# Second layer of an attention and Mamba block: dt goes through DRAM to the decay instead of through TensorE

## The chip, the core and the metric
The kernel runs on one core of one Trainium2 chip. The metric is the device time of one execution in microseconds. The core has five engines with instruction streams of their own: TensorE (PE, matmuls; its weight loads are listed as PEld), VectorE (DVE), ScalarE (ACT), GpSimd (POOL), and SyncE (SP), which here only issues DMA transfers. They are ordered among each other by semaphores. PSUM is the memory that TensorE writes, in 8 banks of 128 partitions x 512 float32; SBUF is the large on-chip memory.

## The reference
Input x is (4, 128, 64, 64) float32. Layer 0 is attention over the 4096 pixels with 4 heads, a residual and a layer norm; its result is z. Layer 1 adds a 3x3 convolution, a spectral convolution (FFT, 1x1, inverse FFT) and a Mamba block over the pixels as a sequence. The change touches the Mamba block:

```
xi, z = split(in_proj_w @ u);  xs = silu(conv1d(xi))          # 256 channels
dt = softplus(dt_proj_w @ x_dbl[:8] + dt_proj_b)              # 256 channels
A = -exp(A_log)                                               # 256 x 16 states
h = exp(dt * A) * h + dt * B * xs                             # for each channel and state, over 4096 positions
y = sum over states of h * C, + xs * D;  out = out_proj_w @ (y * silu(z))
```

## The kernel before
Layer 0 fills the first part of the time, layer 1 the rest; they don't overlap. Layer 1 (the function `layer1`) cuts each of the 4 images into 8 chunks of 512 positions, so it has NIT = 32 steps. In a step the recurrence is worked off in G = 32 groups. A group holds 8 channels x 16 states on the 128 partitions: partition p has channel p // 16 and state p % 16.

For each group g of step `it`:

- TensorE repeats each channel's u = dt * xs on its 16 partitions with a selection matrix, into one of NU = 3 PSUM banks (`repeat_u`, L995), and dt likewise into the single bank DT_BANK (`repeat_dt`, L988), LEAD = 4 groups ahead. Both read a split form: `s_dt` and `s_u` hold a high part and the rest, one on each half of the partitions, in a rounded float32 format, so that one pass of each suffices.
- ScalarE makes the decay `d_a` = exp(a_neg * dt) from DT_BANK into a ring of NDA = 8 tiles (`decay`, L1103). It also copies the last state of group g - 6 into `carry` (L1094), which waits for that group's scan.
- VectorE multiplies u by B in PSUM (`times_b`, L1175), one group ahead of the scan, and then scans (L1189): hh = d_a * hh + that product, along the 512 positions.
- GpSimd multiplies hh by C (L1218), and TensorE sums the states of 4 groups at a time (`sum_states`, L972).

Between the groups of step `it`, the functions `prepare(it + 1, ...)` of each engine work out the inputs of the next step, each piece at a fixed group number written out by hand. For dt on ScalarE: relu and abs in groups 19 and 20, Exp in 21, Ln in 22. On VectorE: dt = relu + ln in group 20 (semaphore `dt_sum`), ux = dt * xs in group 21. The split is made by `high` on ScalarE (L1045) and `low` on VectorE (L1140), in groups 25 and 26 for dt, 27 and 28 for u. In group 10 ScalarE makes two silus between two loads of its function table (L1039, L1040), having waited until VectorE has added the last half of the step before (`y_added`, VectorE's group 5). The convolutions and the output projection are further matmuls on TensorE in the gaps (`fill`, `fill_g`, `out_proj`).

The order on each engine is the order of the code. On TensorE a group is: repeat_u(g), prepare, sums and fills, repeat_dt(g + 4). repeat_dt waits until the decay of the group before has read DT_BANK (`da_ready`), repeat_u until the scan three groups back has freed its bank (`scanned`). The first two steps are written out, the other 30 run in a hardware loop of two steps. SP loads the chunk z of step it + 2 once TensorE has finished with the buffer (`z_used`, group 28 of step it), and stores each finished output; it too has a loop.

Of the kernel before, what the change touches and what calls it, by code (L numbers as in the profile page):

```python
# [673 lines left out]
ST = 16  # L674
GC = 128 // ST
INNER = 2 * C
# [8 lines left out]
def layer1(nc, z_ext, w, out, nb=B):  # L685
# [13 lines left out]

    NIT = nb * STEPS  # L700
    with ExitStack() as ctx:
        def sb(name, shape, dt=F32):
# [9 lines left out]
        ps = ctx.enter_context(nc.psum_tensor("ps1", [128, 8, CH], F32))  # L712
        DT_BANK, U_BANK, Y_BANK, O_BANK, ITEM_BANK = 0, 1, 4, 5, 6
        NU = 3
        win = sb("win", [C, 2 * INNER])
# [23 lines left out]
        gz = sb("gz", [128, 2, 2, LC])  # L739
        s_dt = sb("s_dt", [128, 2, 4, LC], F32R)  # L740
        s_u = sb("s_u", [128, 2, 4, LC], F32R)
# [10 lines left out]
        yt = sb("yt", [128, 2, LC])  # L752
        NDA, NHH, NHC = 8, 8, 8
        d_a = sb("d_a", [128, NDA, LC])
# [7 lines left out]
        with nc.Block() as block:  # L762
# [27 lines left out]
            def _(dve):  # L790
# [23 lines left out]
        (z_in, flipped, item, item_read, sp_log, dt_sum, u_prod, hi_ready, lo_ready,  # L814
         dt_rep, u_rep, da_ready, bu_ready, scanned, kept, hc_ready, y_done, y_added, gated, z_used, o_ready, o_copied,
         o_full, o_even, o_odd) = [sem(x) for x in (
             "z_in", "flipped", "item", "item_read", "sp_log", "dt_sum", "u_prod",
             "hi_ready", "lo_ready", "dt_rep", "u_rep", "da_ready", "bu_ready", "scanned", "kept", "hc_ready", "y_done",
             "y_added", "gated", "z_used", "o_ready", "o_copied", "o_full", "o_even", "o_odd")]


        XS, XD, DT, BI, CI, GATE, GI, NITEM = 0, 2, 3, 5, 6, 7, 9, 10
        G = GROUPS
        LEAD = 4

# [10 lines left out]

        def u_bank_free(it, g):

            before = g - NU if g >= NU else max(k for k in range(G) if k % NU == g % NU) - G
            return it * G + before + 1  # L840

# [11 lines left out]
        with nc.Block() as block:  # L853
            @block.sync
            def _(sp):
                def load(j, p):

                    jw = j if isinstance(j, int) else j % NIT
                    b, lc = jw // STEPS, jw % STEPS

                    ge(sp, z_used, j - 1)
                    ge(sp, flipped, 2 * j)
                    sp.dma_start(za[:, p, :], z_ext[b, :, bass.ds(lc * LC, HALO)]).then_inc(z_in, 16)
                    sp.dma_start(zp[:, p, :, 1:W + 1], z_ext[b, :, bass.ds(lc * LC, HALO)].rearrange("c (h w) -> c h w", w=W)).then_inc(z_in, 16)

                    last = (STEPS - 1 - lc) * LC + W
                    sp.dma_start(stage_j[:, 0:ROWS - 1, :], z_ext[b, :, bass.ds(last + W, LC - W)].rearrange("c (h w) -> c h w", w=W)).then_inc(z_in, 16)
                    sp.dma_start(stage_j[:, ROWS - 1, :], z_ext[b, :, bass.ds((STEPS - lc) % STEPS * LC + W, W)]).then_inc(z_in, 16)

                def store(j, p):  # L870
                    b, lc = j // STEPS, j % STEPS
                    sp.wait_ge(o_full, j + 1)
                    sp.dma_start(out[b, :, bass.ds(lc * LC, LC)], o_sb[:, p, :]).then_inc((o_even, o_odd)[p], 16)

                load(0, 0)
                load(1, 1)
                load(2, 0)
                with sp.Fori(1, NIT // 2) as k:
                    store(k * 2 - 2, 0)
                    load(k * 2 + 1, 1)  # L880
                    store(k * 2 - 1, 1)
                    load(k * 2 + 2, 0)
                store(NIT - 2, 0)
                store(NIT - 1, 1)

                sp.wait_ge(o_even, 16 * (NIT // 2))
                sp.wait_ge(o_odd, 16 * (NIT // 2))
                sp.wait_ge(z_in, 64 * (NIT + 1))

            @block.tensor  # L890
            def _(pe):
# [90 lines left out]

                def repeat_dt(it, p, g):
                    s, j = column(g)
                    if g == 0:
                        pe.wait_ge(lo_ready, it * 4 + 2)
                    ge(pe, da_ready, it * G + g)
                    nc.tensor.matmul(ps[:, DT_BANK, :], sel_g[:, j, :], s_dt[:, p, s, :], start=True, stop=True).then_inc(dt_rep, 1)  # L988

                def repeat_u(it, p, g):  # L990
                    s, j = column(g)
                    if g == 0:
                        pe.wait_ge(lo_ready, it * 4 + 4)
                    ge(pe, scanned, u_bank_free(it, g))
                    nc.tensor.matmul(ps[:, U_BANK + g % NU, :], sel_g[:, j, :], s_u[:, p, s, :], start=True, stop=True).then_inc(u_rep, 1)  # L995
# [3 lines left out]
                def emit(it, p):  # L999
                    for g in range(G):  # L1000
                        if isinstance(it, int) and it == g == 0:
                            for d in range(LEAD):
                                repeat_dt(it, p, d)
                        repeat_u(it, p, g)
# [10 lines left out]
                        if g >= 8 and g % 4 == 0:  # L1015
                            sum_states(it, g // 4 - 2)
                        if g + LEAD < G:
                            repeat_dt(it, p, g + LEAD)
                        else:
                            repeat_dt(it + 1, 1 - p, g + LEAD - G)  # L1020

# [8 lines left out]
            def _(act):  # L1030
# [16 lines left out]
                def prepare(j, p, g):  # L1047
# [12 lines left out]
                    elif g in (19, 20):  # L1060

                        h = g - 19
                        if h == 0:

                            ge(act, lo_ready, j * 4)
                        nc.scalar.activation(dt[:, h, :], take(j, DT + h), ACT.Relu, bias=cols[:, 2 + h:3 + h])
# [9 lines left out]
                    elif g in (25, 26):  # L1076
                        act.wait_ge(dt_sum, j + 1)
                        high(j, p, s_dt, dt, g - 25)
                    elif g in (27, 28):
                        act.wait_ge(u_prod, j + 1)  # L1080
                        high(j, p, s_u, ux, g - 27)
                    elif g == 29:
# [41 lines left out]
                def tail():  # L1124

                    for g in range(LEAD - 1):
                        decay(NIT, g)
                    for g in range(G - KEEP, G):
# [6 lines left out]
            def _(dve):  # L1135
                def low(j, p, stack, src, part, n):

                    a, b = slice(64 * part, 64 * part + 64), slice(64 - 64 * part, 128 - 64 * part)
                    dve.wait_ge(hi_ready, j * 4 + 2 * n + part + 1)
                    nc.vector.tensor_tensor(stack[b, p, part::2, :], src[a, :, :], stack[a, p, part::2, :].bitcast(F32), ALU.subtract  # L1140
                                            ).then_inc(lo_ready, 1)

                def prepare(j, p, g):
# [161 lines left out]
```

## Time and profile before

| | us |
|---|---|
| median of 3 runs | 6361.38 (6359.47 to 6361.48) |
| profiled execution | 6361.27 |
| its span, first to last instruction | 6359.3 |
| mean granted TensorE clock | 0.955 of 2.4 GHz |
| TensorE busy in the span | 5868.1 (92%) |
| VectorE busy | 5011.0 (79%) |
| GpSimd busy | 4188.6 (66%) |
| ScalarE busy | 3777.6 (59%) |

The profile is one execution recorded by the hardware. An engine's busy time is the sum of its instructions without overlap; the difference to the span is idle time. For each idle stretch the profile names what ended it, inferred from the semaphores. Shares over the whole span mix the two layers, so the numbers that matter here are those of the second layer alone, which a window in time gives.

### The profile page before, as it was taken

Reading aid. Unit: us, or ns where it says so; the run is one execution under the profiler, and the core shown is the slowest. Engines: PE = TensorE matmul, PEld = TensorE weight load, DVE = VectorE, ACT = ScalarE, POOL = GpSimd, SP = SyncE. Lnnn points to the kernel's source line nnn. Section 1 sums busy time; section 2 is a strip of 40 time slices with the busy share of each in tenths; the row PEclk is TensorE's granted clock in tenths of the full one; section 3 lists DMA queues with packets and bytes.
Section 4 is the critical chain, followed back from the end, with each engine's and each line's share of the span. In section 5 each row is a group of like instructions: output and inputs, shape, how many; then the busy total and the mean of one; then the engine's idle time right before and its main releaser. Section 6 shows DMA issues by size and latency. Waiting matters only on the chain. (4 is left out here: it accounts for less than half of the span.)

```text
span 6359.3 us, 93797 instructions
## 1 busy us (share of the span) xinstructions
PE 5868.1 (92%) x28212; PEld 2757.3 (43%) x28212; DVE 5011.0 (79%) x7254; ACT 3777.6 (59%) x7359; POOL 4188.6 (66%) x3147
## 2 busy tenths in 40 slices
PE   7999999999999999999999997888888888888887
PEld 3444444444444444444444442333333333333333
DVE  7777777777777777777777773798999998899988
ACT  3666566656666666666666665655556655556655
POOL 2677766776666776666677764566666666666666
PEclk9999999999999999999999998898989998889988
DMA  4011011011011011011000001000000000000000
GB/s 128 22 38 41 26 32 41 25 41 42 26 32 36 29 42 39 27 32 31 14 21 22 9 17 41 15 22 16 15 15 17 15 21 15 15 15 17 15 21 11
DMA packets 143428, 175.15 MB, mean 28 GB/s; under 512 B 64832, under 2 KB 88256, under 8 KB 141504
## 3 DMA queue, kind: packets, MB, share of 16 engines
q1 hardware_dynamic: 142944, 169.73, 9.4%
q8 instruction: 178, 2.92, 0.2%
q14 instruction: 306, 2.51, 0.1%
HBM read 109.11 MB, written 58.98 MB: 26 GB/s over the span
## 5 line engine op out<-in xcount | busy, mean ns | idle before, releaser
L560 POOL TENSOR_TENSOR sums<-exps 128x512 f32<-128x512 f32 x2048 | 2620.2, 1302 | 1309.9 <-ACT exps L493 1305.2
L569 DVE TENSOR_REDUCE mpart<-ps 128x1 f32<-128x512 f32 x4096 | 2539.8, 682 | 820.7 <-PE ps L369 820.7
L493 ACT ACTIVATE exps<-ps 128x512 f32<-128x512 f32 x4096 | 2127.8, 602 | 1404.5 <-PE ps L376 1404.1
L1218 POOL TENSOR_TENSOR hc<-hh,c_rep 128x512 f32<-128x512 f32 x1024 | 1490.0, 1458 | 825.8 <-DVE hh L1189 824.9
L369 PE MATMUL ps<-k_st,q_ring 96*128 96x512 f32 x4096 | 1753.7, 429 | 19.0 <-DMA k_st<-qk_split 9.4
L376 PE MATMUL ps<-q_ring,k_st 98*128 98x512 f32 x4096 | 1621.0, 397 | 4.0 <-ACT exps L493 3.6
L1189 DVE TENSOR_TENSOR_SCAN hh<-d_a,carry,ps 128x512 f32<-128x512 f32 x1024 | 1297.6, 1270 | 2.1
L369 PEld LDWEIGHTS ps<-k_st,q_ring 96*128 96x128 f32 x4096 | 774.7, 189 | 1065.6 <-DVE mpart L569 529.4
L1103 ACT ACTIVATE d_a<-ps,a_neg 128x512 f32<-128x512 f32 x1027 | 706.6, 688 | 726.3 <-PE ps L988 688.3
L387 PE MATMUL ps<-exps,v_ring 128*32 128x512 f32 x8192 | 1090.8, 605 | 0.0
L988 PE MATMUL ps<-s_dt,sel_g 128*128 128x512 f32 x1028 | 638.6, 621 | 324.0 <-ACT d_a L1103 319.7
L1175 DVE TENSOR_TENSOR ps<-ps,b_rep 128x512 f32<-128x512 f32 x1024 | 698.1, 682 | 216.7 <-PE ps L995 201.2
L376 PEld LDWEIGHTS ps<-q_ring,k_st 98*128 98x128 f32 x4096 | 778.0, 190 | 148.3 <-ACT exps L493 17.3
L988 PEld LDWEIGHTS ps<-s_dt,sel_g 128*128 128x128 f32 x1028 | 215.8, 210 | 973.8 <-ACT d_a L1103 747.4
L995 PE MATMUL ps<-s_u,sel_g 128*128 128x512 f32 x1024 | 467.0, 456 | 72.6 <-DVE hh L1189 72.5
L399 PE MATMUL ps<-sums,ones_d 128*32 128x512 f32 x4096 | 533.1, 592 | 0.0
L387 PEld LDWEIGHTS ps<-exps,v_ring 128*32 128x32 f32 x8192 | 161.2, 108 | 416.2 <-ACT exps L493 362.0
L908 PE MATMUL ps<-za,wtap 128*128 128x512 f32 x528 | 285.9, 637 | 28.6 <-DMA stage_j<-z_ext 28.6
L972 PE MATMUL ps<-hc,sel_y 128*32 128x512 f32 x2048 | 299.9, 660 | 4.6 <-POOL hc L1218 4.6
L995 PEld LDWEIGHTS ps<-s_u,sel_g 128*128 128x128 f32 x1024 | 223.1, 218 | 166.1 <-DVE hh L1189 114.2
L954 PE MATMUL ps<-zp,wconv 128*128 128x512 f32 x576 | 278.3, 592 | 0.0
L399 PEld LDWEIGHTS ps<-sums,ones_d 128*32 128x32 f32 x4096 | 133.0, 110 | 306.6 <-issue 296.8
(110 smaller groups left out, 3409.0 us busy)
## 6 DMA issues: line engine op xcount, KB each, us to landing
qk_split<-hilo SPq DMA_DIRECT2D x128, 256.0 KB, 2.3
q_ring<-qk_split SPq DMA_DIRECT2D x384, 64.0 KB, 2.0
k_st<-qk_split SPq DMA_DIRECT2D x45, 512.0 KB, 7.2
za<-z_ext SPq DMA_DIRECT2D x33, 320.0 KB, 3.1
zp<-z_ext SPq DMA_DIRECT2D x33, 320.0 KB, 4.0
xc<-in_x SPq DMA_DIRECT2D x32, 256.0 KB, 3.0
v_dram<-v_stage SPq DMA_DIRECT2D x32, 256.0 KB, 2.3
v_ring<-v_dram SPq DMA_DIRECT2D x16, 512.0 KB, 3.8
```

Source lines behind the costliest of these rows:

```text
L369: nc.tensor.matmul(d_bank(("max", m, t)), q_ring[0:PARTS, m % 4, 128 * i:128 * i + 128], k_st[0:PARTS, g % 2, chunk(kc)], start=True, stop ...
L376: nc.tensor.matmul(a_bank(("exp", n, t)), k_st[0:SHIFT, n // NCH % 2, 128 * t:128 * t + 128], q_ring[0:SHIFT, n % 4, :], start=True, stop= ...
L387: ins = nc.tensor.matmul(ps[D * i:D * i + D, OUT_BANK, :], v_ring[:, n // NCH % 2, 4 * v + i, :], exps[:, (2 * v + i // 2) % 4, CH * (i % ...
L493: nc.scalar.activation(exps[:, u % 4, CH * half:CH * half + CH], a_bank(("exp", n, t)), ACT.Exp, scale=SCALE).then_inc(a_done, 1)
L560: pool.tensor_tensor(sums[:, u % 8, :], exps[:, u % 4, 0:CH], exps[:, u % 4, CH:2 * CH], ALU.add).then_inc(summed, 1)
L569: nc.vector.tensor_reduce(mpart[:, m % 2, t % 4, t // 4:t // 4 + 1], d_bank(("max", m, t)), AX.X, ALU.max).then_inc(d_done, 1)
L988: nc.tensor.matmul(ps[:, DT_BANK, :], sel_g[:, j, :], s_dt[:, p, s, :], start=True, stop=True).then_inc(dt_rep, 1)
L995: nc.tensor.matmul(ps[:, U_BANK + g % NU, :], sel_g[:, j, :], s_u[:, p, s, :], start=True, stop=True).then_inc(u_rep, 1)
L1103: nc.scalar.activation(d_a[:, g % NDA, :], ps[:, DT_BANK, :], ACT.Exp, scale=a_neg[:, s * 8 + j:s * 8 + j + 1]).then_inc(da_ready, 1)
L1175: nc.vector.tensor_tensor(bu, bu, b_rep[:, p, :], ALU.mult).then_inc(bu_ready, 1)
L1189: nc.vector.tensor_tensor_scan(hh[:, g % NHH, :], d_a[:, g % NDA, :], ps[:, U_BANK + g % NU, :], carry[:, it % STEPS, s * 8 + j:s * 8 + j ...
L1218: pool.tensor_tensor(hc[:, g % NHC, :], hh[:, g % NHH, :], c_rep[:, p, :], ALU.mult).then_inc(hc_ready, 1)
```

## The change
dt no longer goes through TensorE. When VectorE has made the dt of a step (all 256 channels x 512 positions), SP stores it to a DRAM tensor `dt_dram` with two halves, one for each parity of the step (`store_dt`). For each group SP then loads the 8 channels of that group back, each channel to 16 neighbouring partitions, straight into the tile of `d_a` that the decay will use (`load_dt`); ScalarE's Exp works in place there. The ring `d_a` grows from 8 to 16 tiles, with one semaphore for each tile. The load for group g + 16 is issued when the scan of group g is done; SP's program is written out in full for this, without a loop, with the z loads at group 26 and the output store at group 18. `repeat_dt`, its PSUM bank, `s_dt` and its `high` and `low` parts go away; u gets a fourth PSUM bank, and its split moves to groups 25 and 26. `repeat_u` then waits for the scan four groups back.

```diff
-        DT_BANK, U_BANK, Y_BANK, O_BANK, ITEM_BANK = 0, 1, 4, 5, 6
-        NU = 3
+        U_BANK, Y_BANK, O_BANK, ITEM_BANK = 0, 4, 5, 6
+        NU = 4
-        NDA, NHH, NHC = 8, 8, 8
+        NDA, NHH, NHC = 16, 8, 8
...
+                def store_dt(j, p):
+                    sp.wait_ge(dt_sum, j + 1)
+                    sp.dma_start(dt_dram[p].rearrange("(h q) l -> q h l", h=2), dt[:, :, :]).then_inc(dt_stored, 16)
+
+                def load_dt(j, p, g):
+                    if g == 0:
+                        sp.wait_ge(dt_stored, j * 16 + 16)
+                    c = channels(g)
+                    sp.dma_start(d_a[:, g % NDA, :], dt_dram[p, c:c + GC, :].rearrange("c (o l) -> c o l", o=1).to_broadcast([GC, ST, LC])
+                                 ).then_inc(dt_in[g % NDA], 16)
+
+                def emit(it, p):
+                    for t in range(G):
+                        if t == G - NDA:
+                            store_dt(it + 1, 1 - p)
+                        sp.wait_ge(scanned, it * G + t + 1)
+                        if t + NDA < G:
+                            load_dt(it, p, t + NDA)
+                        else:
+                            load_dt(it + 1, 1 - p, t + NDA - G)
+                        if t == 18 and it:
+                            store(it - 1, 1 - p)
+                        if t == 26 and it + 2 <= NIT:
+                            load(it + 2, p)
...
-                def repeat_dt(it, p, g):
-                    s, j = column(g)
-                    if g == 0:
-                        pe.wait_ge(lo_ready, it * 4 + 2)
-                    ge(pe, da_ready, it * G + g)
-                    nc.tensor.matmul(ps[:, DT_BANK, :], sel_g[:, j, :], s_dt[:, p, s, :], start=True, stop=True).then_inc(dt_rep, 1)
...
-                    ge(pe, scanned, u_bank_free(it, g))
+                    ge(pe, scanned, it * G + g - NU + 1)
...
-                            ge(act, lo_ready, j * 4)
+                            ge(act, u_prod, j)
+                            ge(act, dt_stored, j * 16)
...
-                        act.wait_ge(dt_sum, j + 1)
-                        high(j, p, s_dt, dt, g - 25)
-                    elif g in (27, 28):
                         act.wait_ge(u_prod, j + 1)
-                        high(j, p, s_u, ux, g - 27)
+                        high(j, p, s_u, ux, g - 25)
...
-                    act.wait_ge(dt_rep, it * G + g + 1)
-                    ge(act, scanned, it * G + g - NDA + 1)
-                    nc.scalar.activation(d_a[:, g % NDA, :], ps[:, DT_BANK, :], ACT.Exp,
+                    act.wait_ge(dt_in[g % NDA], it * (16 * G // NDA) + 16 * (g // NDA) + 16)
+                    nc.scalar.activation(d_a[:, g % NDA, :], d_a[:, g % NDA, :], ACT.Exp,
...
-                        low(j, p, s_dt, dt, g - 25, 0)
-                    elif g in (27, 28):
-                        low(j, p, s_u, ux, g - 27, 1)
+                        low(j, p, s_u, ux, g - 25)
```

## Rows read from the trace of the kernel before

**Rows 1.** The page: the span in 40 slices, VectorE busy and the granted TensorE clock.
```profile
DVE  7777777777777777777777773798999998899988
...
PEclk9999999999999999999999998898989998889988
```
**Rows 2.** Timeline of VectorE (start us, us, engine, line): first and last scan.
```profile
4013.75 1.27 DVE L1189 TENSOR_TENSOR_SCAN hh<-d_a,carry,ps 128x512 f32<-128x512 f32 x1
...
6342.87 2.44 DVE L1189 TENSOR_TENSOR_SCAN hh<-d_a,carry,ps 128x512 f32<-128x512 f32 x2
```
**Rows 3.** Window 4100 to 6200 us: busy (count) of PE, PEld, DVE, ACT, POOL, clock, DMA share, GB/s.
```profile
4100.00:6200.00 2100.00, 1743.10 (x5973) 793.08 (x5971) 1904.23 (x2098) 1243.85 (x2556) 1405.06 (x976) 0.90 0.06 17
```
**Rows 4.** Instruction groups, 4100 to 6200 us: busy us, mean ns, idle before and releaser.
```profile
L1218 POOL TENSOR_TENSOR hc<-hh,c_rep 128x512 f32<-128x512 f32 x919 | 1338.8, 1460 | 693.8 <-DVE hh L1189 692.9 <-PE ps L972 0.9
L1189 DVE TENSOR_TENSOR_SCAN hh<-d_a,carry,ps 128x512 f32<-128x512 f32 x920 | 1165.9, 1270 | 1.9
L1103 ACT ACTIVATE d_a<-ps,a_neg 128x512 f32<-128x512 f32 x919 | 632.3, 688 | 656.0 <-PE ps L988 618.2 <-DVE hh L1189 32.8 <-issue 2.8
...
L988 PE MATMUL ps<-s_dt,sel_g 128*128 128x512 f32 x919 | 572.6, 623 | 292.3 <-ACT d_a L1103 288.3
...
L1140 DVE TENSOR_TENSOR s_dt<-dt,s_dt 64x1024 fp32r<-64x1024 f32 x58 | 70.7, 1220 | 1.8
```
**Rows 5.** Waits, 4100 to 6200 us: us in total, times, longest.
```profile
ACT d_a L1103 <- PE ps L988: 618.2, 630, 4.4
...
DVE ps L1175 <- PE ps L995: 175.9, 142, 2.4
```
**Rows 6.** Timeline of VectorE: scans around an s_dt subtraction, and without one.
```profile
5014.81 1.28 DVE L1189 TENSOR_TENSOR_SCAN hh<-d_a,carry,ps 128x512 f32<-128x512 f32 x1
...
5017.98 1.27 DVE L1189 TENSOR_TENSOR_SCAN hh<-d_a,carry,ps 128x512 f32<-128x512 f32 x1
...
5035.81 1.27 DVE L1189 TENSOR_TENSOR_SCAN hh<-d_a,carry,ps 128x512 f32<-128x512 f32 x1
...
5037.59 1.27 DVE L1189 TENSOR_TENSOR_SCAN hh<-d_a,carry,ps 128x512 f32<-128x512 f32 x1
```
**Rows 7.** Timeline of ScalarE, TensorE, VectorE about group 10; idle time before in brackets.
```profile
5044.90 1.28 ACT L1039 ACT_TABLE_LOAD   x1 [1.54 <-DVE yt L1160]
...
5048.78 0.69 ACT L1103 ACTIVATE d_a<-ps,a_neg 128x512 f32<-128x512 f32 x1
...
5049.52 0.50 PE L988 MATMUL ps<-s_dt,sel_g 128*128 128x512 f32 x1 [3.40 <-ACT d_a L1103]
...
5050.29 0.70 DVE L1175 TENSOR_TENSOR ps<-ps,b_rep 128x512 f32<-128x512 f32 x1 [1.93 <-PE ps L995]
```
**Rows 8.** Timeline of the second layer's start: the dt sum and the first decay.
```profile
3995.37 1.23 DVE L1146 TENSOR_TENSOR dt<-dt,edt 128x1024 f32<-128x1024 f32 x1 [25.57 <-ACT edt L1073]
...
4006.93 0.69 ACT L1103 ACTIVATE d_a<-ps,a_neg 128x512 f32<-128x512 f32 x1
```
**Rows 9.** DMA: a 256 KB load; windows over reads, narrow loads, a store, z loads.
```profile
xc<-in_x SPq DMA_DIRECT2D x32, 256.0 KB, 3.0
...
178.70:184.50 5.80, 5.80 (x37) 2.75 (x37) 4.18 (x9) 3.52 (x8) 4.89 (x4) 1.00 0.27 81
...
329.00:336.00 7.00, 7.00 (x41) 3.39 (x41) 5.76 (x12) 4.46 (x9) 4.96 (x4) 1.00 1.04 223
...
5068.60:5071.60 3.00, 2.98 (x11) 1.21 (x12) 3.00 (x4) 3.00 (x7) 2.32 (x2) 1.00 0.23 87
5091.30:5097.00 5.70, 4.43 (x37) 3.62 (x30) 5.57 (x7) 2.02 (x5) 3.90 (x3) 1.00 0.64 161
```
**Rows 10.** Windows of 2.4 us: the clock (third column from the end) low, and back.
```profile
5101.60:5104.00 2.40, 2.32 (x9) 0.49 (x9) 1.78 (x3) 0.00 (x0) 2.30 (x2) 0.50 0.00 0
...
5108.80:5111.20 2.40, 2.40 (x9) 1.24 (x7) 2.40 (x3) 1.25 (x3) 1.28 (x2) 1.00 0.01 3
```

More of the change, by code:

```diff
@@ L700, in layer1 @@
     NIT = nb * STEPS
+    dt_dram = nc.dram_tensor("dt_dram", [2, INNER, LC], F32, kind="Internal").ap()
     with ExitStack() as ctx:
@@ L739, in layer1 @@
         gz = sb("gz", [128, 2, 2, LC])
-        s_dt = sb("s_dt", [128, 2, 4, LC], F32R)
         s_u = sb("s_u", [128, 2, 4, LC], F32R)
@@ L814, in layer1 @@
         (z_in, flipped, item, item_read, sp_log, dt_sum, u_prod, hi_ready, lo_ready,
-         dt_rep, u_rep, da_ready, bu_ready, scanned, kept, hc_ready, y_done, y_added, gated, z_used, o_ready, o_copied,
-         o_full, o_even, o_odd) = [sem(x) for x in (
+         u_rep, da_ready, bu_ready, scanned, kept, hc_ready, y_done, y_added, gated, z_used, o_ready, o_copied,
+         o_full, o_even, o_odd, dt_stored) = [sem(x) for x in (
              "z_in", "flipped", "item", "item_read", "sp_log", "dt_sum", "u_prod",
-             "hi_ready", "lo_ready", "dt_rep", "u_rep", "da_ready", "bu_ready", "scanned", "kept", "hc_ready", "y_done",
-             "y_added", "gated", "z_used", "o_ready", "o_copied", "o_full", "o_even", "o_odd")]
+             "hi_ready", "lo_ready", "u_rep", "da_ready", "bu_ready", "scanned", "kept", "hc_ready", "y_done",
+             "y_added", "gated", "z_used", "o_ready", "o_copied", "o_full", "o_even", "o_odd", "dt_stored")]
+        dt_in = [sem(f"dt_in{i}") for i in range(NDA)]
         XS, XD, DT, BI, CI, GATE, GI, NITEM = 0, 2, 3, 5, 6, 7, 9, 10
         G = GROUPS
-        LEAD = 4
         def ge(e, s, value):
@@ L835, in column, with channels @@
             return 2 * half + i // 2, jj + 4 * (i % 2)
-        def u_bank_free(it, g):
-            before = g - NU if g >= NU else max(k for k in range(G) if k % NU == g % NU) - G
-            return it * G + before + 1
+        def channels(g):
+            half, jj, i = g // 16, g // 4 % 4, g % 4
+            return 128 * half + 32 * i + GC * jj
         def steps(e, prepare, emit, tail):
@@ L856, in load @@
                 def load(j, p):
-                    jw = j if isinstance(j, int) else j % NIT
+                    jw = j % NIT
                     b, lc = jw // STEPS, jw % STEPS
@@ L873, in store @@
                     sp.dma_start(out[b, :, bass.ds(lc * LC, LC)], o_sb[:, p, :]).then_inc((o_even, o_odd)[p], 16)
+                def store_dt(j, p):
[20 more added lines that the diff above has]
+                            load(it + 2, p)
                 load(0, 0)
                 load(1, 1)
[L877 to L883, printed above, removed]
+                store_dt(0, 0)
+                for g in range(NDA):
+                    load_dt(0, 0, g)
+                for it in range(NIT):
+                    emit(it, it % 2)
                 store(NIT - 1, 1)
@@ L887, in _ @@
                 sp.wait_ge(o_odd, 16 * (NIT // 2))
+                for i in range(NDA):
+                    sp.wait_ge(dt_in[i], 16 * (NIT * G // NDA + 1))
                 sp.wait_ge(z_in, 64 * (NIT + 1))
@@ L992, in repeat_u @@
                     if g == 0:
-                        pe.wait_ge(lo_ready, it * 4 + 4)
-                    ge(pe, scanned, u_bank_free(it, g))
+                        pe.wait_ge(lo_ready, it * 2 + 2)
+                    ge(pe, scanned, it * G + g - NU + 1)
                     nc.tensor.matmul(ps[:, U_BANK + g % NU, :], sel_g[:, j, :], s_u[:, p, s, :], start=True, stop=True).then_inc(u_rep, 1)
@@ L1000, in emit @@
                     for g in range(G):
-                        if isinstance(it, int) and it == g == 0:
-                            for d in range(LEAD):
-                                repeat_dt(it, p, d)
                         repeat_u(it, p, g)
@@ L1016, in emit @@
                             sum_states(it, g // 4 - 2)
[L1017 to L1020, printed above, removed]
                 def tail():
@@ L1124, in tail @@
                 def tail():
-                    for g in range(LEAD - 1):
-                        decay(NIT, g)
                     for g in range(G - KEEP, G):
@@ L1135, in _, with low @@
             def _(dve):
-                def low(j, p, stack, src, part, n):
+                def low(j, p, stack, src, part):
                     a, b = slice(64 * part, 64 * part + 64), slice(64 - 64 * part, 128 - 64 * part)
-                    dve.wait_ge(hi_ready, j * 4 + 2 * n + part + 1)
+                    dve.wait_ge(hi_ready, j * 2 + part + 1)
                     nc.vector.tensor_tensor(stack[b, p, part::2, :], src[a, :, :], stack[a, p, part::2, :].bitcast(F32), ALU.subtract
```

## The prediction

> **What bounds the kernel now.** The change touches only the second layer, so I first looked in the page's forty slices for where that layer lies: from the 26th slice on, where VectorE (DVE) is at 8 to 9 tenths and the granted clock of TensorE at 8 to 9 tenths [rows 1]. The first scan starts at 4013.75 us and the last ends at 6342.87 + 2.44 = 6345.31 us [rows 2]. That is 2331.6 us for 32 steps of 32 groups, 72.86 us a step. Then one window over the steady part, 4100 to 6200 us, which is 2100 / 72.86 = 28.82 steps: DVE is busy for 1904 of 2100 us, TensorE 1743, ScalarE 1244, GpSimd 1405, the DMA engines 6% [rows 3]. Per step that is DVE 66.1 us and 6.8 us idle. So DVE is nearly the bound, but not quite, and the list of waits tells what the rest is: DVE's multiplication by B waits 175.9 us for TensorE's repeat of u, 6.1 us a step, and this is nearly all of its idle time. In the same list ScalarE's decay waits 618 us for TensorE's repeat of dt [rows 5].
>
> The timeline shows how the two hang together. TensorE issues in order: repeat of u for group g, other work, repeat of dt for group g+4. That dt repeat may only start when the decay of g+3 has read the one dt bank. ScalarE makes two table loads and two silus in group 10, so the decay of group 11 comes late, at 5048.78 us. TensorE has stood idle for 3.40 us when its dt repeat starts at 5049.52; the u repeat queued behind it is later still, and DVE's product starts at 5050.29 after 1.93 us of idleness [rows 7]. The decays themselves are far ahead of the scan: no scan waits for one (1.9 us of idle time before 920 scans [rows 4]). DVE waits for u only because u stands in the queue behind dt.
>
> **What the change removes.** (1) On TensorE 32 dt repeats a step of 0.623 us, 19.9 us a step [rows 4]. TensorE isn't the bound, so this counts for nothing by itself; what counts is that the coupling is gone. A u repeat then waits only for the scan four groups back (a fourth bank; three before), while DVE needs it when the scan two groups back ends. That is a margin of two groups, 2 x 1.77 us, against in-line work of mostly 0.9 to 2 us a group.
> (2) On DVE the two subtractions into s_dt. From scan start to scan start takes 5037.59 - 5035.81 = 1.78 us without an extra operation and 5017.98 - 5014.81 = 3.17 us with one s_dt subtraction [rows 6]. So each costs 1.40 us on the path, a little more than its 1.22 us [rows 4], and the two 2.8 us a step. DVE's work a step becomes 66.1 - 2.8 = 63.3 us. This is the floor.
> (3) On ScalarE two casts a step and one of the two waits of each decay. ScalarE is busy 1244 / 28.82 = 43.2 us a step [rows 3]; worth nothing on the path. The Exp reads SBUF in place of PSUM. Bounds for one: 0 and 0.69 us as now [rows 4]; I take it as unchanged, and even +0.1 us on each would leave ScalarE at 46 us.
>
> **What it adds.** (4) On the SP queue 32 loads of 256 KB a step, one store of 512 KB, and a wait for the scan before each load. The load of group g+16 starts when scan g is done; ScalarE can't run more than six groups ahead of the scan (its copies of the last state are in the same stream), so a load has ten groups, some 20 us, to land. A load of 256 KB lands in 3.0 us now [rows 9]. The awkward place is t = 16: the store of the next step's dt stands first there and waits for the dt sum, which DVE makes after scan 20. Queued behind it on SP are the loads of groups 0 to 4 of the next step, and then the wait for the store. They go out in a burst at about scan 21 or 22 and are wanted from scan 31 on; with 3 us for the store, 3 us for the first load and under 2 us for each further one, nothing is late. The z loads now stand at t = 26 behind that scan, where they waited for TensorE's fill of group 28 before. They land 6 us later, when TensorE may stand for some 2 us at group 1 of the next step, inside the margin of (1).
> (5) The DMA engines' throughput is the real unknown, since no row of before has this form: eight rows of 2 KB in DRAM, each written to 16 partitions. Per packet of 2 KB the store of 256 KB took 0.23 x 3.0 us x 16 engines = 11.0 engine-us for 128 packets, 86 ns; the reads from 178.7 us took 0.27 x 5.8 x 16 = 25.1 engine-us for 0.47 MB, 53 us per MB, so 14 engine-us for 256 KB [rows 9]. Spread over 16 engines a load takes 0.69 to 0.88 us, over 8 engines 1.38 to 1.75 us. The low end is 0.69. For the high end I take the loads of 329 to 336 us, whose destinations are 32 partitions only: all engines busy, but 223 GB/s in all, 13.9 GB/s an engine [rows 9]. If only 8 engines work, at this rate, 32.8 KB each take 2.35 us. Beside them the step has the z loads (0.64 x 5.7 = 3.65 us of all engines [rows 9]), the output (0.69) and the dt store (twice that, 1.38): 5.7 us. So the DMA needs 28 to 34 us a step on 16 engines, 50 to 62 on 8, and 81 on 8 that get in each other's way; DVE needs 63.3. I take 50 to 62, under DVE's floor, nearest to the plain reads and stores.
>
> The Trainium skill, page "DMA: Bandwidth & Descriptors", section "Why a DMA increments its semaphore by 16 and not by 1", says that a copy is spread over the largest number up to 16 that divides the slowest dimension of both sides; here these are 8 and 128, so 8 engines. No row here shows such a copy; by that rule 1.38 us and up holds, not 0.69. The page "SBUF — State Buffer", section "Door 1: The DMA port swizzle", says that partitions reach the 16 DMA ports in a pattern, so that a narrow range has only some of them; the trace agrees for the 32-partition loads (223 GB/s). Together they would make the last rival below.
>
> (6) Start: dt is summed at 3995.37 + 1.23 = 3996.60 us and the first decay ran at 4006.93 [rows 8]. Store and first load need about 6 us, so dt is there by about 4003, before ScalarE comes to it. The first scan then no longer waits for five dt repeats and decays in turn; it can start near 4006.9, 7 us earlier than at 4013.75.
>
> **The sum.** The profiled execution took 6361.27 us, its span 6359.3; the median of the runs is 6361.38, the same within 0.1 us. Of the 6.8 us idle a step I leave 0.7: TensorE still falls to 1.2 GHz after idle stretches (0.50 at 5101.6 us [rows 10]) and is then slow for some 7 us, which eats most of the margin of two groups once or twice a step. Step = 63.3 + 0.7 = 64.0 us, saving 8.86 x 32 = 283.5 us, and 7 us at the start: 6361.3 - 290.5 = 6071 us. By itself this case lies between 6045 (no stall left) and 6130 (2.5 us left).
>
> **Rivals.**
> A. The DMA is the bound but still quicker than now: 1.8 to 2.1 us a load, for instance 1.95: 32 x 1.95 + 5.7 = 68.1 us a step, 6361.3 - 7 - 32 x 4.76 = 6202 us. For it: the high end of the plain reads, 1.75 us on 8 engines, is only just below the 1.79 us from which DMA exceeds DVE. Against: the stores at 86 ns.
> B. The DMA makes the kernel slower: 8 engines, each at the 13.9 GB/s of the narrow loads, 2.35 us a load, 81 us a step, and scans then wait for decays and these for loads: 6361.3 - 7 + 32 x 8.1 = 6614 us. It decides from 2.10 us a load on (32 x 2.10 + 5.7 = 72.9), 125 GB/s. For it: each channel goes to 16 neighbouring partitions, so several engines may write at once where the narrow loads met. Against: in one load all 128 partitions are written.
> C. TensorE keeps stalling DVE, by its clock. Without the dt repeats it is busy 60.5 - 19.9 = 41 us of 64, so it idles more and is granted 1.2 GHz for longer; u would then be late as now. Price: the 6.1 us of waits stay, 69.4 us a step: 6361.3 - 7 - 32 x 3.46 = 6244 us. Against: where TensorE is behind it is busy without a gap, and after such a stretch the clock was back: 0.50 from 5101.6 us, 1.00 from 5108.8 us [rows 10].
> GpSimd is no rival: 1.46 us a group [rows 4] against 1.97.
>
> **How the numbers follow.** Forecast 50%, A 15%, C 8%, B 25%, no change (something not seen gives it all back) 2%. The predicted time is 6071. Under 0.2% (13 us) a measurement of this kernel can't tell from no change. Faster: 50 + 15 + 8 = 73%; same 2%; slower 25%. The range runs from 6040 into case B until a fifth is left out, to 6480; the likeliest case's own range is 6045 to 6130.
>
> **What would show it.** Right: no TensorE group that writes ps from s_dt; DVE above 97% busy in the second layer, with scans 64 us x 32 in sum; no wait of a decay for a DMA apart from the start; DVE's wait for u down from 175.9 us to under 30 in the same stretch; a mean DMA share of 0.43 to 0.53 in the second layer ((32 x 11 to 14 + 16 x 5.7) engine-us of 16 x 64). Wrong: ScalarE's decay waiting for d_a from dt_dram and time from issue to landing growing far above 3 us (A or B; the rate tells which), or DVE still waiting for ps of L995's counterpart with a clock at 0.8 or less (C).

## The result, and the profile after

The changed kernel takes 6183.6 us, the median of 4 runs from 6175.5 to 6202.5; the kernel before took 6360.4 beside it. The ratio is 0.9727, with a 95% interval of 0.9704 to 0.9749. That is 177 us less, where 290 were forecast: the way and the stated range (6040 to 6480) are right, but the time lies outside the likeliest case's own range (6045 to 6130). It lies in the stated range only because that was stretched for rivals A to C, and none of them came about: that part is luck. The profiled execution took 6181.0 us, its span 6179.2.

The page of the changed kernel, its span in 40 slices: VectorE, the granted TensorE clock, the DMA engines.
```profile
DVE  7777777777777777777777777299999999999998
PEclk9999999999999999999999999899899889988998
DMA  4011011111110110110100000244444444444444
```
VectorE now shows 9 tenths nearly throughout the second layer (8 and 9 in [rows 1]), and the DMA engines 4 tenths.

The timeline of the changed kernel's VectorE (start, us, engine, line): first and last scans.
```profile
4006.75 1.27 DVE L1195 TENSOR_TENSOR_SCAN hh<-d_a,carry,ps 128x512 f32<-128x512 f32 x1
...
6162.16 2.44 DVE L1195 TENSOR_TENSOR_SCAN hh<-d_a,carry,ps 128x512 f32<-128x512 f32 x2
```
The first scan is 7.0 us earlier than in [rows 2]. Between the ends lie 6164.60 - 4006.75 = 2157.9 us, 67.43 us a step; before it was 72.86. So 32 x 5.43 + 7.0 = 181 us, which is the whole difference of the two profiled executions (6361.3 - 6181.0 = 180).

The window of the steady part, 4100 to 6000 us (898 scans, so 28.06 steps of 67.7 us), its columns as in [rows 3], and then its costliest groups.
```profile
4100.00:6000.00 1900.00, 1459.61 (x4938) 592.63 (x4940) 1774.28 (x1993) 1165.38 (x2441) 1313.06 (x954) 0.90 0.45 150
```
```profile
L1224 POOL TENSOR_TENSOR hc<-hh,c_rep 128x512 f32<-128x512 f32 x898 | 1246.8, 1392 | 587.3 <-DVE hh L1195 584.9 <-PE ps L999 2.4
L1195 DVE TENSOR_TENSOR_SCAN hh<-d_a,carry,ps 128x512 f32<-128x512 f32 x898 | 1136.6, 1268 | 0.9
L1113 ACT ACTIVATE d_a<-d_a,a_neg 128x512 f32<-128x512 f32 x898 | 642.0, 720 | 76.0 <-issue 74.6
L1181 DVE TENSOR_TENSOR ps<-ps,b_rep 128x512 f32<-128x512 f32 x898 | 605.9, 678 | 123.1 <-issue 64.2 <-PE ps L1016 57.6
```
VectorE is busy 1774.28 / 28.06 = 63.2 us a step; 63.3 was forecast. The idle time is where the forecast fails: 125.7 / 28.06 = 4.5 us a step, not 0.7. The list of waits of the same window (total us, times, longest) divides it, and shows who else waits.
```profile
ACT s_u L1059 <- DVE ux L1157: 154.4, 28, 5.6
PE ps L935 <- DMA stage_j<-z_ext: 146.7, 28, 8.1
ACT zj L1066 <- DMA stage_j<-z_ext: 131.5, 28, 7.5
...
ACT d_a L1113 <- issue: 74.6, 13, 6.2
DVE ps L1181 <- issue: 64.2, 19, 4.9
...
DVE ps L1181 <- PE ps L1016: 57.6, 39, 5.1
```
The decays no longer wait for TensorE (618 us in [rows 5]), and no line of the whole list shows one waiting for a dt load. VectorE's wait for u has fallen from 175.9 to 57.6 us. New are waits of TensorE and ScalarE for the z load (`stage_j`), once in every step, and waits called "issue" in every second step: 13 of ScalarE's in 28 steps, 5.7 us each, and at the same places 13 of VectorE's, 59.9 of its 64.2 us, so 4.6 us each. "Issue" is what the profile calls a wait for which it sees no releaser.

The timeline of SP in one step shows why z is late.
```profile
5057.93 0.37 SPq L878 DMA_DIRECT2D dt_dram<-dt  x1
5060.81 1.82 SPq L884 DMA_DIRECT2D d_a<-dt_dram  x3
5062.67 0.46 SPq L873 DMA_DIRECT2D out<-o_sb  x1
5063.17 9.16 SPq L884 DMA_DIRECT2D d_a<-dt_dram  x8
5072.43 0.40 SPq L863 DMA_DIRECT2D za<-z_ext  x1
5072.88 0.43 SPq L864 DMA_DIRECT2D zp<-z_ext  x1
5073.36 4.78 SPq L867 DMA_DIRECT2D stage_j<-z_ext  x1
5078.18 0.43 SPq L868 DMA_DIRECT2D stage_j<-z_ext  x1
```
The dt store goes out late, when the dt sum is made. Eleven loads that have become due follow in a burst, and SP is held to their pace: eight of them take 9.16 us to issue. Only then come the z loads, and one of these holds SP for 4.78 us more. From issue to landing the larger `stage_j` load takes 9.3 us here (median), and 3.8 us in the kernel before. The burst's pace is plain at the start of the layer. This is the DMA view of 4020 to 4040 us:
```profile
DMA packets 2083, 4.01 MB, mean 201 GB/s; under 512 B 124, under 2 KB 124, under 8 KB 2083
...
q1 hardware_dynamic: 2083, 4.01, 52.5%
```
A share of 52.5% is about that of eight of the 16 engines, and 262144 B / 201 GB/s = 1.30 us a load, below the 1.38 to 1.75 us of the prediction's term (5) and far from the 2.35 of rival B.

The timelines of ScalarE, VectorE and TensorE at the start of two consecutive steps, idle time before in brackets.
```profile
5017.38 2.07 PE L935 MATMUL ps<-za,wtap 128*128 128x512 f32 x2 [5.34 <-DMA stage_j<-z_ext]
...
5019.91 0.70 DVE L1181 TENSOR_TENSOR ps<-ps,b_rep 128x512 f32<-128x512 f32 x1 [3.12 <-PE ps L1016]
...
5077.76 0.72 ACT L1113 ACTIVATE d_a<-d_a,a_neg 128x512 f32<-128x512 f32 x1 [5.54 <-issue]
...
5084.41 0.20 ACT L1066 COPY zj<-stage_j 128x8 f32<-128x8 f32 x1 [3.73 <-DMA stage_j<-z_ext]
...
5086.09 1.30 DVE L1181 TENSOR_TENSOR ps<-ps,b_rep 128x512 f32<-128x512 f32 x2 [4.71 <-issue]
```
At the first, TensorE stands for 5.34 us for z, u is late behind it, and VectorE loses 3.12 us. At the second, ScalarE and VectorE stand for 5.54 and 4.71 us for nothing that the profile names. This second kind lies where the hardware loop of two steps jumps back.

What the engines wait for there can be seen among the DMA queues. They have one more, called "instruction", with packets of 8 KB. This is its line in the DMA view of 5072.3 to 5077.7 us, the stretch in which ScalarE stands:
```profile
q14 instruction: 1, 0.01, 0.6%
```
That one packet ends at 5076.25 us, and ScalarE goes on 1.51 us later. In all 13 such waits of ScalarE between 4100 and 6000 us a packet of this queue ends 1.43 to 1.58 us before the engine goes on, and in all 13 of VectorE's one ends 1.82 to 1.88 us before. In the kernel before it is 1.24 to 1.52 us for ScalarE's 12, whose waits are only 2.4 to 2.9 us long. So the engines stand for their instructions, and what has grown is the time until the packet is there.

### The profile page after: what moved, and what is told of

Read it like the earlier page. It is cut to its first block and busy times, and to the rows that moved or that the text cites. A ratio compares the mean times of both kernels' runs of the same rounds, so it can differ in the third digit from the quotient of the medians.

```text
span 6179.2 us, 90944 instructions
## 1 busy us (share of the span) xinstructions
PE 5589.3 (90%) x27184; PEld 2550.2 (41%) x27184; DVE 4912.2 (79%) x7188; ACT 3717.1 (60%) x7290; POOL 4118.1 (67%) x3147
## 5 line engine op out<-in xcount | busy, mean ns | idle before, releaser
L1224 POOL TENSOR_TENSOR hc<-hh,c_rep 128x512 f32<-128x512 f32 x1024 | 1422.0, 1393 | 713.1 <-DVE hh L1195 710.7
L1016 PE MATMUL ps<-s_u,sel_g 128*128 128x512 f32 x1024 | 665.6, 650 | 232.6 <-DVE hh L1195 230.5
L1113 ACT ACTIVATE d_a<-d_a,a_neg 128x512 f32<-128x512 f32 x1024 | 732.0, 720 | 85.8 <-issue 79.7
L1016 PEld LDWEIGHTS ps<-s_u,sel_g 128*128 128x128 f32 x1024 | 210.1, 205 | 832.6 <-DVE hh L1195 671.6
L935 PE MATMUL ps<-za,wtap 128*128 128x512 f32 x528 | 333.5, 732 | 187.9 <-DMA stage_j<-z_ext 187.9
L1106 ACT COPY carry<-hh 128x1 f32 (+1 forms) x1024 | 187.5, 183 | 304.6 <-DVE hh L1195 303.8
L981 PE MATMUL ps<-zp,wconv 128*128 128x512 f32 x576 | 297.4, 627 | 0.0
L935 PEld LDWEIGHTS ps<-za,wtap 128*128 128x128 f32 x528 | 119.3, 233 | 288.8 <-issue 243.8
```

Source lines behind the costliest of these rows:

```text
L1113: nc.scalar.activation(d_a[:, g % NDA, :], d_a[:, g % NDA, :], ACT.Exp, scale=a_neg[:, s * 8 + j:s * 8 + j + 1]).then_inc(da_ready, 1)
L1224: pool.tensor_tensor(hc[:, g % NHC, :], hh[:, g % NHH, :], c_rep[:, p, :], ALU.mult).then_inc(hc_ready, 1)
```

## The experiments

Theory: the 4.5 us a step have two causes. Z loads come late behind the burst of dt loads, and after each jump back an engine has to fetch instructions, which takes longer beside the dt traffic. Main rival: the eight DMA engines are simply the bound. All times below are medians of 4 runs (10 for the shorter lead). They come from three chips, and a ratio is to the kernel before on the same chip (6365.8, 6359.5 and 6362.7 us), so differences of some 5 us between two experiments are not told apart by the times. Where the traces are finer, the text gives the time from one dt sum of VectorE to the next, which is one step.

**Early z loads.** `za` and `stage_j` of step it + 2 are loaded at t = 5, `zp` stays at t = 26 with a semaphore of its own.
```diff
-                        if t == 26 and it + 2 <= NIT:
-                            load(it + 2, p)
+                        if t == 5 and it + 2 <= NIT:
+                            load(it + 2, p)           # za, stage_j
+                        if t == 26 and it + 2 <= NIT:
+                            load_zp(it + 2, p)
...
+                            pe.wait_ge(zp_in, it * 16 + 16)     # at the first fill
```


> Change: za and stage_j of step it + 2 are loaded at t = 5 of step it instead of t = 26; zp stays at t = 26 with a semaphore of its own, for which TensorE waits at its first fill. Theory (the residual idleness of VectorE has two causes, late z loads and slow instruction fetch at the loop's jump back): the waits of TensorE and ScalarE for stage_j (147 and 132 us of the changed kernel between 4100 and 6000 us) go, and with them VectorE's wait for ps of the u repeat, 57.6 us there, 66 us over 32 steps; its idle time called issue, 64 us, stays. About 6115 us. Rival (the eight DMA engines are the bound): the same bytes move through the same engines, so no gain, 6170 to 6190 us, and the idle time turns into waits of the decay.

Measured: 6114.6 us, ratio 0.9608 (0.9592 to 0.9624). The first cause is shown, 69 us between the medians (the changed kernel's own runs lie up to 27 us apart); the mean step falls from 67.75 to 65.64 us. The list of waits of VectorE, 4100 to 6000 us, has one line left:
```profile
DVE ps L1191 <- issue: 72.0, 28, 4.7
```
Three dt sums of its VectorE in a row show the second cause by itself:
```profile
5021.59 1.19 DVE L1164 TENSOR_TENSOR dt<-dt,edt 128x1024 f32<-128x1024 f32 x1
...
5090.26 1.20 DVE L1164 TENSOR_TENSOR dt<-dt,edt 128x1024 f32<-128x1024 f32 x1
...
5153.40 1.19 DVE L1164 TENSOR_TENSOR dt<-dt,edt 128x1024 f32<-128x1024 f32 x1
```
A step with a jump back takes 68.7 us (68.0 to 68.8 in all 14), one without 63.14. The same bytes through the same eight engines take no time in the second kind of step, so the rival falls.

**Loop written out.**
```diff
-            for it in range(2):
-                emit(it, it)
-            with e.Fori(1, NIT // 2) as k:
-                for r in range(2):
-                    emit(k * 2 + r, r)
+            for it in range(NIT):
+                emit(it, it % 2)
```


> Change: the hardware loop of two steps on TensorE, VectorE, ScalarE and GpSimd is written out, 32 steps in a row. Theory of slow fetch at the jump back: VectorE's idle time called issue (64 us between 4100 and 6000, 4.7 us at every second step's start) goes; but at those starts the late z loads would then show, as they do at the others (3.4 us and 0.3), so about 1 us for every second step is won at least and 4.7 at most: 6105 to 6165 us. If the idle time is not instruction fetch but a late transfer: unchanged, 6175 to 6200 us.

Measured: 6158.1 us, ratio 0.9678 (0.9661 to 0.9694), 25 us less than the changed kernel. VectorE has no wait "issue" any more, nor has any decay, and the late z shows instead, as expected, where the jump had covered it:
```profile
DVE ps L1178 <- PE ps L1013: 97.8, 52, 7.9
```

**Loads over 16 engines.** Each channel is stored twice, so that a group reads 16 rows.
```diff
-    dt_dram = nc.dram_tensor("dt_dram", [2, INNER, LC], F32, kind="Internal").ap()
+    dt_dram = nc.dram_tensor("dt_dram", [2, INNER, 2, LC], F32, kind="Internal").ap()
...
-   dt_dram[p, c:c + GC, :].rearrange("c (o l) -> c o l", o=1).to_broadcast([GC, ST, LC])
+   dt_dram[p, c:c + GC, :, :].rearrange("c r (o l) -> (c r) o l", o=1).to_broadcast([2 * GC, ST // 2, LC])
```


> Change: dt is stored twice, each channel in two rows, so that a group's load reads 16 rows and writes each to 8 partitions. If a load uses as many engines as divide both outer sizes, it now runs on 16 at once, and a burst of loads moves at about 16 x 25 = 400 GB/s or what the memory gives, not 200; the burst ahead of the z loads is over in half the time and z lands before it is wanted. Then most of the 57.6 us go: about 6110 to 6130 us. If the width of the transfers does not matter: 6175 to 6195 us, with 200 GB/s still in the burst.

Measured: 6086.7 us, ratio 0.9564 (0.9548 to 0.9580), better than forecast. Windows of this kernel in the first burst, and VectorE's waits, 4100 to 6000 us:
```profile
4010.00:4015.00 5.00, 4.58 (x13) 1.90 (x11) 5.00 (x7) 3.98 (x10) 3.52 (x4) 1.00 1.06 265
```
```profile
DVE ps L1182 <- issue: 31.4, 10, 4.4
DVE ps L1182 <- PE ps L1017: 12.9, 5, 3.3
```
All 16 engines work now, but move 265 GB/s and not 400. With that third more VectorE waits for u only 5 times in the window, though TensorE still waits for z a little (26.1 us, 146.7 before). The line "issue" has halved too, and ScalarE's 14 waits at the jumps take 4.0 us each and not 5.7, though the loop is as it was: their length hangs on what the DMA engines carry beside them.

The rule of the Trainium skill weighed in the prediction (page "DMA: Bandwidth & Descriptors", section "Why a DMA increments its semaphore by 16 and not by 1": the number of engines is the largest up to 16 that divides both outer sizes) agrees with both kernels: 52.5% of 16 engines busy for outer sizes 8 and 128, all of them for 16 and 128.

**A ring of 8.**
```diff
-        NDA, NHH, NHC = 16, 8, 8
+        NDA, NHH, NHC = 8, 8, 8
```


> Change: the ring of d_a has 8 tiles, so a load is issued 8 groups ahead, and the dt store stands at t = 24, after the dt sum is long done. Theory of the burst: SP no longer stands for 9.5 us at t = 16 waiting for the dt sum, no burst of 13 loads precedes the z loads, and they land 4 to 8 us earlier: 6110 to 6150 us. Rival: the ring of 16 is needed to cover the transfers; with 8 only two groups, 3.5 us, are left beyond ScalarE's lead of six, decays wait for their loads, and the time is over 6200 us.

Measured: 6118.3 us, ratio 0.9616 (0.9600 to 0.9632). The waits of this kernel, 4100 to 6000 us:
```profile
ACT d_a L1113 <- DMA d_a<-dt_dram: 418.7, 454, 4.5
...
DVE ps L1181 <- PE ps L1016: 33.4, 27, 4.1
DVE ps L1181 <- issue: 32.7, 17, 4.2
```
The decays do wait for their loads, as the rival said, half of them, but ScalarE was ahead, and no scan waits for it. With the store at t = 24 three loads and not eleven stand between it and the z loads, and SP is no longer held for the dt sum. Z is earlier, but not yet in time: TensorE still waits 75.5 us for it (146.7 in the changed kernel) and VectorE 33.4 us for u. The ring of 16 was not needed for this speed: it made the burst.

**Both causes away, and all three edits.** The first two edits together, and those with the third.

> Change: the early z loads (za and stage_j at t = 5) and the loop written out together. Theory of the two causes: neither of VectorE's waits is left, it works without a gap, 63.1 us a step; from the first scan at 4006.8 us 32 x 63.1 = 2019 us, and 16.4 us for the tail: 6042 us, and at most 6050. If something third stands behind (the eight DMA engines, TensorE's clock) it shows now as waits of VectorE, and the time stays above 6060 us.

Measured: 6045.4 us, ratio 0.9503 (0.9487 to 0.9518).

> Change: early z loads, loop written out, and the loads over 16 engines. If VectorE is the bound once both causes are gone, the wider loads bring nothing more: within 5 us of the kernel with the first two, 6040 to 6048 us. If the DMA engines still cost something there: faster than it by more than 10 us.

Measured: 6040.0 us, ratio 0.9496 (0.9480 to 0.9512). The window of the first of these, 4100 to 6000 us; VectorE has no line in the list of waits at all.
```profile
4100.00:6000.00 1900.00, 1515.56 (x5298) 598.64 (x5298) 1896.22 (x2138) 1260.55 (x2623) 1412.30 (x1024) 0.96 0.47 160
```
VectorE is busy for 99.8%, and that is what shows that nothing third stands behind the two causes. Taken in this order they bring 69.0 us (early z) and 6114.6 - 6045.4 = 69.2 us (loop). These two must add up to the 138.2 us between 6183.6 and 6045.4, so the sum proves nothing, and the split hangs on the order: with the loop written out first it is 25.5 us for the loop and 112.7 for z, since each stall covers part of the other. The wider loads bring nothing more that these runs show: the medians lie 5 us apart, and a step takes 63.14 us in both traces.

**The kernel before with its loop written out.**

> Change: the kernel before, its loop written out (all but SP's). Without the traffic of the dt loads the fetch at the jump back costs VectorE only 12.4 us of idle time between 4100 and 6200 us, 14 us over 32 steps: 6346 to 6362 us. If the jump back itself were the cost and not the traffic beside it, the gain would be like that of the changed kernel, 25 us or more, so under 6335 us.

Measured: 6314.3 us, ratio 0.9927 (0.9911 to 0.9944): a miss, 45 us where 14 at most were expected. I had counted only VectorE's own idle time. ScalarE stood at each jump as well, and in this kernel the dt chain can hand that on to VectorE. The timeline of the kernel before, one jump, ScalarE:
```profile
4876.68 0.69 ACT L1103 ACTIVATE d_a<-ps,a_neg 128x512 f32<-128x512 f32 x1 [2.85 <-issue]
```
At the other jumps the profile puts ScalarE's stall down to a scan, and with the loop written out no decay has such a wait. So the jump is dear without the traffic too, 45.2 / 15 = 3.0 us for each of the 15 passes of the loop (with 14 jumps between them), and with it and the early z loads 69.2 / 15 = 4.6 us.

This kernel, free of the jumps, also shows a part of the waits for u that has nothing to do with dt. VectorE and TensorE where a step begins:
```profile
5007.50 2.44 DVE L1186 TENSOR_TENSOR_SCAN hh<-d_a,carry,ps 128x512 f32<-128x512 f32 x2
5008.92 0.77 PE L992 MATMUL ps<-s_u,sel_g 128*128 128x512 f32 x1 [3.10 <-DVE hh L1186]
...
5012.07 0.63 PE L992 MATMUL ps<-s_u,sel_g 128*128 128x512 f32 x1
...
5012.74 0.70 DVE L1172 TENSOR_TENSOR ps<-ps,b_rep 128x512 f32<-128x512 f32 x1 [2.20 <-PE ps L992]
```
The bank of u is g % 3, counted anew in every step, and 3 does not divide 32. So group 0 takes the bank of group 30 and group 1 that of group 31: their repeats wait for the scan two groups back, not three. TensorE stands for 3.10 us until scan 30 is done, then works at half its clock (0.50 from 5009 to 5012.5 us), and u of group 1 is late. Group 1 has 29 of the 144 waits for u in the window here, 63.5 of 149.3 us, and 28 of 142 in the kernel before, 44.0 of 175.9 us. With the changed kernel's four banks it is always the scan four groups back, and group 1 has no wait.

**A shorter lead in the kernel before.**
```diff
-        LEAD = 4
+        LEAD = 2
```


> Change: the kernel before with LEAD = 2 instead of 4, so that the u repeat stands behind the dt repeat of two groups ahead and not of four. Theory (VectorE waits for u only because u is queued behind dt, which waits for a late decay): at group 10 the margin grows by two groups, 3.5 us, and of the 6.1 us a step 2 to 4.5 go: 6215 to 6300 us, without any DMA. Rival: a lead of two is too short, scans wait for decays instead, and the time is that of before or more, 6355 us and up.

Measured: 6370.0 us, ratio 1.0015 (1.0005 to 1.0025). The rival's time holds, but not its mechanism, since no scan waits for a decay. The waits, 4100 to 6200 us:
```profile
ACT d_a L1103 <- PE ps L988: 831.9, 645, 6.8
...
DVE ps L1175 <- PE ps L995: 174.9, 158, 2.1
```
ScalarE waits longer for dt (618 before) and VectorE as long for u (175.9 in [rows 5]). The waits do follow the queue: the largest in the kernel before stands at group 9 (62.5 us in the window), here at group 11 (42.3 us), and in both u stands behind the dt repeat of group 12. What the shorter lead wins there comes back elsewhere, at groups 12, 13 and 25. Why it does is not shown; the reading is that dt and decay follow each other through one bank, and a shorter lead leaves the decays less ahead.

**TensorE's time put back without a wait**, on the kernel with early z and no loop.
```diff
+   nc.tensor.matmul(ps[:, U_BANK + g % NU, :], sel_g[:, j, :], s_u[:, p, s, :], start=True, stop=True)
    nc.tensor.matmul(ps[:, U_BANK + g % NU, :], sel_g[:, j, :], s_u[:, p, s, :], start=True, stop=True).then_inc(u_rep, 1)
```


> Change, on the kernel with early z loads and the loop written out: each u repeat is issued twice into the same bank, so TensorE does again what the dt repeats cost it, 0.5 to 0.65 us a group, and nothing waits for anything more. If what the change took away was the coupling (u queued behind a dt repeat that waits for a decay) and not TensorE's time, VectorE stays without waits: within 10 us of 6045. If TensorE's busy time was what made u late: VectorE's waits for u come back, up to 6.1 us a step as in the kernel before, 6100 to 6240 us.

Measured: 6040.4 us, ratio 0.9495 (0.9479 to 0.9511). Its window, 4100 to 6000 us:
```profile
4100.00:6000.00 1900.00, 1671.51 (x6263) 777.76 (x6262) 1896.21 (x2137) 1260.50 (x2619) 1417.45 (x1024) 0.98 0.47 160
```
TensorE is busy for 1672 us, not 1516, and VectorE loses nothing. That puts back 5.2 us a step of TensorE's time, where 60.5 - 50.4 = 10.1 us had gone since the kernel before, so at least this half was worth nothing. The other half is not tested, nor is the fourth bank, which all these kernels have.

**The two subtractions put back**, on the same kernel, into a tile that nobody reads.
```diff
+                    elif g in (27, 28):
+                        part = g - 27
...
+                        nc.vector.tensor_tensor(s_x[b, p, part::2, :], ux[a, :, :], s_u[a, p, part::2, :].bitcast(F32), ALU.subtract)
```


> Change, on the same kernel: the two VectorE subtractions a step that the change took away are put back in groups 27 and 28, writing a tile that nobody reads. By the prediction's second term each costs 1.40 us on the path when VectorE is the bound: 6045 + 32 x 2.8 = 6135 us. If they had been hidden in waits: 6045 to 6060 us.

Measured: 6129.0 us, ratio 0.9636 (0.9620 to 0.9652). They cost 83.6 us, 1.31 us each by the medians, which come from two chips. In the traces a step grows from 63.14 to 65.91 us, 1.39 us for each; 1.40 was forecast.

**The product u on GpSimd**, on the kernel with all three edits.
```diff
-                        nc.vector.tensor_tensor(ux[:, :, :], dt[:, :, :], xs[:, p, :, :], ALU.mult).then_inc(u_prod, 1)
+                def product(j, p, g):                       # GpSimd, group 21
+                        pool.tensor_tensor(ux[:, :, :], dt[:, :, :], xs[:, p, :, :], ALU.mult).then_inc(u_prod, 1)
```


> Change, on the kernel with all three edits: the product ux = dt x xs is made by GpSimd instead of VectorE. VectorE is the bound there, and the product costs it about 1.13 us a step: 6040 - 32 x 1.13 = 6004 us, if GpSimd (74% busy) takes the 2.5 us more without making hc late. Rival: u then comes later by GpSimd's queue and longer operation, and shared access of the two engines to SBUF slows VectorE's scans: 6040 us or more.

Measured: 6029.9 us, ratio 0.9478 (0.9462 to 0.9493), the fastest version here, but 10 us won by the medians, and 0.43 us a step or 14 us by the traces (62.71 after 63.14), not 36. Its groups, 4100 to 6000 us:
```profile
L1156 DVE TENSOR_TENSOR s_u<-ux,s_u 64x1024 fp32r<-64x1024 f32 x60 | 94.6, 1576 | 1.9
...
L1243 POOL TENSOR_TENSOR ux<-dt,xs 128x1024 f32<-128x1024 f32 x31 | 73.3, 2365 | 0.0
```
VectorE's subtraction takes 1.58 us on average here and 1.22 in the others. Of the two in a step the second takes 1.22 us as ever, but the first 1.93: GpSimd, late after its product, then works off one multiplication by C after another. That takes back 0.7 us a step of the 1.13.

## Why the prediction was right, and where it failed

- Term (1), TensorE's repeats: the waits for u did go, and half of the busy time, put back, cost nothing (u twice). But the time was put too high: TensorE's busy time fell from 60.5 to 52.0 us a step in the changed kernel, by 8.5 and not by 19.9. "DVE waits for u only because u stands in the queue behind dt" is right for the wait at group 9, which moved with the lead, and wrong in "only": a quarter of the waits (44.0 of 175.9 us) stood at group 1 and came from three banks in a step of 32 groups. So the change did two things at once, dt out of the queue and a fourth bank, and no run has one without the other. No run had a second dt bank either.
- Term (2), 2.8 us a step for the two subtractions: 2.77 by the traces, 2.6 by the medians. The floor of 63.3 us: 63.14 with both stalls away.
- Term (4) failed: "They land 6 us later, when TensorE may stand for some 2 us at group 1 of the next step, inside the margin". I had seen the burst, though with five loads where eleven went out, and reckoned that no dt load in it would be late. But I took the z loads behind it as landing as they did alone, while they queue behind it and SP is held as well (9.3 us to landing and not 3.8). TensorE stood for 5.2 us a step and ScalarE for 4.7, which was not inside the margin. Price 69 us, when it is mended first.
- The jump back of the loop was in no term. In the kernel before it cost 45 us already, hidden in waits that bear other names (ScalarE's 13 waits for VectorE's scan, 32.8 us, in [rows 4] are of this kind: one in every second step, where the scan had long been done). A stall that comes once in two steps where the work is the same in each step was the sign. Price 69 us in the changed kernel, when z is early; 25 us when it is not. Together with z this is the idle time of 4.5 us a step where the sum left 0.7.
- Term (5), 1.38 to 1.75 us a load on eight engines: 1.30. The forecast DMA share of 0.43 to 0.53 was 0.45.
- Term (6), the start 7 us earlier: 7.0.
- Rival A's 6202 us is close to the measured time, but not its mechanism: a load takes 1.30 and not 1.95 us, and no scan waited for the DMA's rate. Rival B (the one that "the last rival below" means) had a wrong price for eight engines by a factor of 1.8. Rival C falls with the early z loads: at a mean clock of 0.92 in the window, hardly above the 0.90 of before, VectorE has no wait for u.
- Of its signs, two held (no wait of a decay for a DMA, the DMA share) and two did not: VectorE was busy for 93% of the steady part and not above 97, and its wait for u was 57.6 us, not under 30. Both point at term (4) and the jump.

The sum as the runs leave it, from 6360.4 to 6045.4 us with both new stalls away: 7 us start, 84 subtractions, 45 the jumps, and 179 left over, 5.6 us a step (6.1 forecast for the waits for u). That last is a remainder. The trace of the kernel before without its loop has 149.3 / 29.3 = 5.1 us a step of such waits, 2.2 of them at group 1, so by the three banks, and the rest by the dt chain or TensorE's other work. Of these 315 us the changed kernel gives 138 back.

## What to carry to other kernels

When a stream of transfers is added to a queue that carries others, reckon the landing of the others behind the longest burst, not of the stream itself; and a wait that holds the queue (here for dt, at t = 16) makes that burst. Issue what is free to go early ahead of it. Look for waits that occur once in a pass of a hardware loop though the work repeats more often, as here in every second step: they point at the jump, and here they grew with the DMA traffic beside them. And where buffers are counted anew in each step, check that their number divides the groups, or the first groups of a step have less room than the rest.

## What the runs showed of the hardware

- The jump back costs 3.0 us a pass in the kernel before and 4.6 beside 154 GB/s in the one with early z. ScalarE's stall at the jump is 2.4 to 2.9 us in the kernel before, and 5.3 to 6.2 in the changed one. The Trainium skill, page "Runtime: NRT & Kernel Launch", section "Instruction fetch mechanics", says that a taken branch to a target outside the small fetched window forces a DMA fetch of it before execution goes on; the trace agrees: each of ScalarE's stalls in both kernels, and of VectorE's in the changed one, holds a packet of the instruction queue that ends 1.2 to 1.9 us before the engine goes on, and the stalls go when the loop is written out.
- GpSimd's product by C takes 1460 ns in the kernel before [rows 4] and 1392 in the changed one, and 1461 again when the two VectorE subtractions are put back. These are means of two kinds: in the changed kernel it takes 1.27 us by itself and 2.22 us where it overlaps one of VectorE's operations on dt and ux with two SBUF inputs, which then keeps its own 1.20 or 1.22 us. The other way round it is the 1.93 us above.
- The Exp from SBUF takes 720 ns, from PSUM it took 688.
- Eight DMA engines moved 201 GB/s, 25 GB/s each, from rows of 2 KB in DRAM to 16 partitions each; sixteen moved 265, with 8 partitions to a row.
- SP is held while the engines are busy: eight dt loads in a burst took it 9.16 us to issue, and one z load behind them 4.78 us, against 0.40 us for the same load in the kernel before.
